# Moving a layer norm's statistics and normalisation by one to two steps, a free step, and one low half between engines, in a two-layer transformer kernel

## The reference

```python
xn = _layernorm(x, axis=-1)
x = x + _L0_attn_ref(xn, ...) + _L0_ffn_ref(xn, ...)
xn = _layernorm(x, axis=-1)
x = x + _L1_attn_ref(xn, ...) + _L1_ffn_ref(xn, ...)
```

## Time and profile before

| what | value |
| --- | --- |
| time, median of 3 runs | 1114.13 us (1113.35 to 1114.25) |
| profiled execution, its own time | 1113.54 us |
| profiled execution, span from first to last instruction | 1111.8 us |
| busy: TensorE, VectorE, ScalarE, GpSimd | 94%, 76%, 62%, 47% |
| chain that ended last, by engine | PE 64%; DVE 13%; POOL 8%; ACT 6%; DMA 4%; issue 3% |
| turns 0 to 3 of layer 0 begin near | 28, 104, 192 and 279 us |

### The profile page before, as it was taken

The page is one execution under the profiler, slowest core; times in us unless marked ns, Lnnn a source line. Parts: engine busy times, 40 slices in busy tenths (PEclk is TensorE's granted clock), DMA queues, the critical chain, the costliest instruction groups (busy, mean ns, idle before and its releaser), DMA issues.

```text
span 1111.8 us, 21342 instructions
## 1 busy us (share of the span) xinstructions
PE 1046.6 (94%) x7339; PEld 956.7 (86%) x7339; DVE 840.2 (76%) x1696; ACT 687.6 (62%) x1922; POOL 519.5 (47%) x626
## 2 busy tenths in 40 slices
PE   8768899899899799999999999999999999999997
PEld 6657779779778688888899999999999999899997
DVE  6676787887867667887777777778777777777776
ACT  3856676766665435555666666766666665555554
POOL 5586665664675000007844454444453443588200
PEclk9999999999999999999999999999999999999999
DMA  7746746746664296624544554445445453333130
GB/s 219 230 129 193 215 142 204 202 153 190 176 211 138 91 261 175 220 87 157 173 139 139 150 203 148 149 134 158 161 140 177 147 163 99 106 100 97 65 114 19
DMA packets 140490, 171.71 MB, mean 154 GB/s; under 512 B 11232, under 2 KB 103520, under 8 KB 139488
## 3 DMA queue, kind: packets, MB, share of 16 engines
q1 hardware_dynamic: 137312, 161.96, 47.7%
q0 software_dynamic: 3072, 8.39, 2.3%
HBM read 121.95 MB, written 48.37 MB: 153 GB/s over the span
## 4 chain that ended last, share of the span: by engine, by line
PE 64%; DVE 13%; POOL 8%; ACT 6%; DMA 4%; issue 3%; SPq 2%; DVEq 0%; POOLq 0%; ACTq 0%
PE ps_m L1703 25%; PE ps_s L1703 9%; PE ps_t L1703 7%; PE ps_b L1703 4%; PE ps_b L849 3%; POOL d_xs L1332 3%; ACT probs L502 2%; PE ps_t L1858 2%; PE ps_c L1858 2%; PE ps_c L1703 2%; DMA d_w_head<-parts 2%; DVE neg_max L791 2%; PE ps_t L916 1%; PE ps_m L849 1%; DMA d_q_scr<-sT 1%
## 5 line engine op out<-in xcount | busy, mean ns | idle before, releaser
L1450 ACT ACTIVATE probs_a<-ps_s,neg_max_a 128x256 f32<-128x256 f32 x256 | 118.0, 473 | 139.6 <-DVE neg_max_a L1667 139.6
L1703 PE MATMUL ps_m<-xTa,w_qk 128*128 128x512 f32 x768 | 199.0, 398 | 4.2 <-DVE v L1519 1.6
L1703 PEld LDWEIGHTS ps_m<-xTa,w_qk 128*128 128x128 f32 x768 | 136.8, 188 | 34.7 <-issue 5.4
L502 ACT ACTIVATE probs<-ps_s,neg_max 128x128 f32<-128x128 f32 (+1 forms) x256 | 104.9, 422 | 55.4 <-DVE neg_max L791 54.2
L1667 DVE TENSOR_REDUCE neg_max_a<-ps_s 128x2 f32<-128x512 f32 x128 | 87.9, 690 | 43.3 <-PE ps_s L1703 41.7
L1349 POOL CAST we_down<-raw_down_e 128x256 fp32r<-128x256 f32 x47 | 18.7, 398 | 208.5 <-DMA raw_down_e<-in_we_down 208.5
L1703 PE MATMUL ps_m<-w_v,xTa 128*128 128x256 f32 x768 | 106.1, 288 | 0.0
L1703 PE MATMUL ps_s<-kTa,qTa 128*128 128x256 f32 x768 | 102.9, 283 | 0.3 <-DVE kTa L1489 0.2
L1703 PE MATMUL ps_t<-pTa,v 128*128 128x256 f32 x762 | 102.8, 284 | 0.0
L1703 PEld LDWEIGHTS ps_s<-kTa,qTa 128*128 128x128 f32 x768 | 96.7, 192 | 1.0 <-DVE kTa L1489 0.7
L1703 PEld LDWEIGHTS ps_t<-pTa,v 128*128 128x128 f32 x762 | 96.2, 191 | 0.1
(11 more groups left out here) (261 smaller groups left out, 2827.9 us busy)
## 6 DMA issues: line engine op xcount, KB each, us to landing
w_qk<-d_w_head SPq DMA_DIRECT2D x64, 512.0 KB, 3.9
raw_up<-in_we_up SPq DMA_DIRECT2D x47, 352.0 KB, 3.6
d_w_head<-parts SPq DMA_DIRECT2D x128, 128.0 KB, 2.6
raw_down_e<-in_we_down SPq DMA_DIRECT2D x47, 256.0 KB, 2.9
codes<-in_w_codes SPq DMA_DIRECT2D x64, 128.0 KB
scales<-in_w_scales SPq DMA_DIRECT2D x64, 128.0 KB
q<-d_q_scr SPq DMA_DIRECT2D x28, 256.0 KB, 5.3
d_xs<-zeros SPq DMA_DIRECT2D x16, 384.0 KB, 5.6
```

The lines of the kernel that those rows point to most:

```text
L502: last = act.activation(probs[:, g % 3, a * w:(a + 1) * w], ps_s[g % 2][:, a * w:(a + 1) * w], ACT.Exp, bias=neg_max[:, g % 2, a:a + 1], s ...
L1450: last = act.activation(probs[:, s, t, :], ps_s[s][:, t * SEQ:(t + 1) * SEQ], ACT.Exp, bias=neg_max[:, s, t:t + 1], scale=1.0, accum_out=s ...
L1703: last = pe.matmul(out, lhs[i], rhs[j], start=start and n == 0, stop=stop and n == 2, skip_group_check=True)
```

## The change

Three edits. First, in turns 0 to 2 the statistics of the next turn's two halves move from steps 11 and 12 to steps 10 and 11, and the normalisation from steps 14 and 15 to steps 12 and 14. Second, in the last turn the free step that was 5 is now 1. Third, the low half of the very last context (g = 99) is computed by VectorE in its woven step and no longer by GpSimd.

```diff
@@ -203,7 +203,7 @@
         if p + 1 < TURNS:
             for half in range(2):
-                ln_stats_at[b + 11 + half] = ln_at[b + 14 + half] = (p + 1, half)
+                ln_stats_at[b + 10 + half] = ln_at[b + 12 + 2 * half] = (p + 1, half)
@@ -233,7 +233,7 @@
-    LAST_FREE = (5, 15, 16)
+    LAST_FREE = (1, 15, 16)
@@ -485,7 +485,7 @@
-            if g in ctx_high_at:
+            if g in ctx_high_at and g < ALL:
                 context_low(*ctx_high_at[g])
@@ -801,6 +801,11 @@
+            if g in ctx_high_at and g >= ALL:
+                p, i = ctx_high_at[g]
+                dve.wait_ge(ctx_high.sem, ctx_high.at(0, TP * p + i + 1))
+                dve.tensor_tensor(cT[1][:, i, :, :].rearrange("p c n -> p (c n)"), ctx_f[:],
+                                  cT[0][:, i, :, :].rearrange("p c n -> p (c n)").bitcast(F32), ALU.subtract).then_inc(ctx_low.sem, 1)
             if g in xn1_at:
```

## The result

The changed kernel takes 1118.58 us (median of 9 runs, 1115.55 to 1120.63). The kernel before, in runs beside it, takes 1113.23 us (9 runs). The ratio is 1.0046, with a 95% interval of 1.0035 to 1.0057: the change makes the kernel slower by 5.35 us. I had forecast 1114.9 us, "same", with 1111.5 to 1116.8 us as the range, so both the time and the side were missed. The profiled execution of the changed kernel took 1120.63 us, so the losses in its trace read some 2 us larger than the median's.

The account below looks back on a forecast made before the run. TensorE, busy 1046.6 us or 94% of the span, was taken as the bound. The terms 1.4 - 0.65 - 0.15 + 0.15 gave +0.75 us, forecast as 1114.9 us, range 1111.5 to 1116.8.

Parts of the forecast that it names:

- (a): Turns 1 and 2, layer norm's move: gated at step 12 comes late, +0.7 us a turn, +1.4 in all.
- the loop: Turns 1 and 2: neg_max, exponentials, tanh, gated, gated_s or sT, TensorE; VectorE work ahead of step 12's neg_max is on it.
- the TensorE row at 152.37, which waits for gated_s, starts 1.3 later: Turn 1: gated's 1.3 us delay was taken to reach this row and all behind it.
- the 0.89 us of step 14's sT: Turns 1 and 2: against 0.68 with GpSimd idle; GpSimd's splits finishing earlier were counted as 0.2 us back.
- absorbed on the way: Turns 1 and 2: of gated's 1.3 us, 0.4 absorbed before step 14's exponentials and 0.2 at sT, leaving 0.7.
- the 1.78 us wait of step 14: Turn 0: TensorE's wait for GpSimd's hT at the output projection, taken to absorb VectorE's extra 0.7 to 1.6 us.
- (b): Turn 0: extra work in steps 10 to 13 absorbed, normalisation leaving step 15 wins; -0.65 us, bounds -1.0 and +0.5.
- (c): Turn 3, free step 1 in place of 5: splits and stores shift, -0.15 us, bounds -0.5 and +0.3.
- (d): Last context's low half on VectorE: TensorE starts at 378.40 against 378.26, +0.15 us, bounds 0 and +0.3.
- Rival A: Slower: turns 1 and 2's delay comes through whole and turn 0's gain is lost; +2.6 us, 1116.7, chance 0.15.
- Rival B: Faster: fewer VectorE and GpSimd collisions in turn 0, turns 1 and 2 free; -2.65 us, 1111.5, chance 0.18.

Follow-up runs that it names:

- e4: The changed kernel with the bias addition of turns 1 and 2 at step 10 instead of 11; 1115.91 against 1112.56 us for the kernel before, ratio 1.0026.
- e1: The kernel before with only the layer norm's move (statistics and normalisation, turns 0 to 2); 1115.96 against 1112.56 us, ratio 1.0036.
- e9: The kernel before with an extra VectorE reduction (14 times 256 columns) ahead of gated at step 12 of turns 1 and 2; 1150.66 against 1145.9 us.
- e6: The kernel before with the layer norm's new places in turn 0 alone; 1145.18 against 1145.9 us, ratio 0.9996.
- e11: The kernel before with the layer norm's new places in turn 0 alone and the bias addition at step 10; 1111.71 against 1113.4 us, ratio 0.9986.
- e14: The kernel before with turn 0's new places, bias addition at step 10, last low half on VectorE ahead of its second probs_a product; 1111.67 against 1113.29 us.
- e5: The changed kernel again, timed on a chip where every kernel takes 3% longer; 1150.72 against 1145.9 us for the kernel before, ratio 1.0042.
- e8: The kernel before with an extra VectorE reduction (10 times 256 columns) ahead of gated at step 12 of turns 1 and 2; 1146.72 against 1145.9 us.

## Why the prediction was wrong

- **(a), the loop.** The reading was right: the neg_max of step 12, gated and gated_s carry the delay to TensorE, and the bias addition blocks xn. I had gated start 1.3 us late, against an entry now 0.87 us early; it starts 0.11 + 0.87 = 1.0 late. The step that failed is the next, "the TensorE row at 152.37, which waits for gated_s, starts 1.3 later". It starts 0.94 + 0.87 = 1.8 us later, because sT between gated and gated_s is held up too, 1.51 us for 0.69; without the hold-ups of xn and sT, in e4, it is 0.8. I had read that very thing in the 0.89 us of step 14's sT, and there counted it as a gain, but I did not follow GpSimd's rows past the bias addition to see its hT land on the sT of step 12.
- The page "SBUF — State Buffer" of the Trainium skill, section "Who interferes with whom", says also that a VectorE operation with two SBUF inputs contends with a GpSimd operation that reads SBUF. sT is one, and its 1.51 us agree. I had used the half of the rule that is on tensor_scalar, and the 2.50 us of xn, ending with the bias addition, agree with that half.
- **What becomes of it.** The wait for gated_s was 2.86 us, and I had written 2.3. At full clock a turn loses 1.19 us (turn 2 of e1) against my +0.7, inside its bounds of 0.1 to 1.3. What I had said is absorbed on the way, 0.6 us, was right in size: 1.8 came in, 1.19 was left, and the wait for sT behind it is 0.7 us shorter than before.
- **The term that was missing**, and the one that carried the time out of my range, is TensorE's clock. I priced a longer wait by its length alone. With 3.4 us at half clock behind it a turn loses 2.6 to 2.9 us and with 6.8 us 3.8. The granted clock around had it: in the kernel before, the 1.78 us wait of step 14 was followed by 3.4 us at half clock (70 to 74 us), and I took that wait for room, not for a warning. e9 shows that the wait is enough. An estimate of the whole from these: the mean granted clock of the nine runs is 0.9932, of the runs of before beside e1 0.9968; over 1117 us that is 4.0 us of clock, or 2.4 falls of 1.7 us more in an execution, which at 1.4 us each cost 3.3. With 2.4 for two turns' waits, 0.2 for the low half, 0.3 for the free step and -0.7 for turn 0 (e6) the sum is +5.5, and 5.35 was measured. So near a match is luck: the -0.7 alone is not told from nothing, and the estimate takes the falls near 30 us, which differ from execution to execution, to be as many in both kernels. Without the 3.3 the nine runs' median would be 1115.3 us, inside the range.
- **(b), turn 0.** -0.65 for the row gone from step 15: the traces have -0.9 to -1.0. What I had not seen is what takes it back: step 2 of turn 1 is 1.3 us longer in the changed kernel's trace than in that of before, and some 0.8 in the mean of all traces, at GpSimd's rstd behind splits behind the store queue. And the 1.78 us of the earlier trace rows, on which I leaned, belong to one execution: the seven of the experiments with the old places that took 19.8 us wait 0.84 to 0.87 us for that hT.
- **(c), the free step.** -0.15 was forecast, +1.15 measured alone, of which the traces show 0.3: the sign was wrong, and 0.3 is the upper edge of my bounds. GpSimd idle at step 5 had been cover for VectorE's xn_t.
- **(d), the last low half.** The wait was right to 0.01 us (1.85 and 1.86). The clock behind it was not in the sum.
- **Rival A** (slower) had the side and was dismissed at 1116.7 with "both turns through whole"; its mechanism, the delay not absorbed, is a part of what happened, and its price was short of the clock as well. Rival B's point, fewer collisions, holds for turn 0 alone: in five of the seven kernels with the new places TensorE's wait for hT at step 14 is gone. e11 and e14 are what it would have needed.

## What to carry to other kernels

Price a wait that gets longer on a nearly full TensorE twice: its length, and, as measured here, some 1.4 us if the granted clock falls behind it, and look in the trace for shorter waits that already have a fall behind them. One trace shows one draw: compare several before a wait or a fall is put into a sum. When a row is moved beside another engine's long one, follow that engine two or three rows further: the row that is held up may be the next one on the critical loop. An idle gap ahead of a critical row is room only for work that can't be held up.

## What the hardware showed

The clock's fall is a matter of chance from execution to execution: the same wait of 2.86 us was followed by 6.8, 3.4 and 0 us at half clock, and waits of 1.86 and 2.27 us by none. The length of the one wait doesn't settle it either: near 62 us, in turn 0, the seven kernels with the new places wait 2.13 to 2.47 us for pT, and the clock fell behind one of these waits (e1). Near 30 us, where no kernel differs from another, the traces have 3.4, 6.8 or 10.2 us at half clock. The page "TensorE: Matmul & The Clock Gate" of the Trainium skill, section "Part 1: The HAM clock gate (the "warmup" mystery)", gives the clock gate two states, 1.2 GHz when idle and 2.4 when busy; the trace agrees with the two levels.

What a fall costs depends on where it lies. In kernels with a wait that is longer than before, slow executions are those with a low mean clock: e4's fastest, 1111.67 us, had 0.997, its four slowest, 1117.11 to 1117.69 us, 0.991 or 0.992. In the kernel before there is no such tie: on one chip its fastest execution, 1111.56 us, had 0.995 and its slowest, 1115.93 us, 0.997. What makes its times spread is not known.

On the chip of e5, e6, e8 and e9 the clock was at half in layer 1, in all four profiled executions, from near 520 us on and for 31 to 38 us, at a place where no kernel differs. Windows of e6 there, then one of the kernel before on the first chip, then a row of e6's timeline of TensorE:

```profile
500.00:520.00 20.00, 15.28 (x111) 1.00 0.45 152
512.00:519.00 7.00, 3.54 (x26) 1.00 0.55 187
520.00:560.00 40.00, 19.73 (x85) 0.57 0.19 69
560.00:600.00 40.00, 39.88 (x288) 1.00 0.41 128
```

```profile
512.00:519.00 7.00, 7.00 (x54) 1.00 0.49 181
```

```profile
516.97 0.94 PE L1704 MATMUL ps_t<-pTa,v 128*128 128x256 f32 x6 [1.08 <-issue]
```

The kernel before on the first chip has 1.00 and 38.42 us busy in 520 to 560. The half clock is not the first thing to go wrong: in e6 TensorE is busy for half of the time from 512 to 519 us, at full clock. It stands there without waiting for anything that the profile shows ("issue"). In all four traces an idle stretch of this kind, of 1.0 to 1.3 us, stands ahead of the fall; between 510 and 565 us they add up to 20.7 to 21.7 us, up to 2.9 us at a time, and the kernel before on the first chip has none. So most of the 33 us between the chips is this idle time, and the slower clock adds to it; what brings it on is not known.
